# A graph kernel whose six gather passes are fetched by GpSimd alone, through a ring of eight waves

## The reference, cut to what matters

```python
# L0, four steps: one row of a table of 3125*4 rows for each edge, summed by destination, then a GRU
m = (embedding @ W_msg.T + b_msg).reshape(n, 4, 128)
r = segment_sum(m[src, etype], dst)
embedding = gru_cell(r, embedding, ...)
# L1: one row of x for each edge, scaled by a small network of the edge's attributes, summed
x_j = x[src]; msg = pe(edge_w) * x_j + x_j
s = segment_sum(msg, dst) / count
# L2: one row of h for each edge, summed, then a GRU
messages = segment_sum(h[src] @ W_msg.T + b_msg + emb[edge_type], dst)
# L3: attention over the edges: rows of k and v (1 KB together) for each edge, softmax by destination
alpha = softmax_by_dst((q[dst] * (k[src] + e)).sum(-1) / 4)
out = segment_sum((v[src] + e) * alpha, dst)
```

## Time and profile before

| what | value |
|---|---|
| median of 3 runs | 4273.61 us |
| lowest and highest | 4272.66 and 4279.78 us |
| profiled execution, first to last instruction (span) | 6447.3 us |
| GpSimd busy in it | 2764.1 us, 43% |
| TensorE busy in it | 2897.1 us, 45% |
| VectorE, ScalarE busy in it | 1811.8 us and 443.4 us |
| granted TensorE clock | 0.699 of 2.4 GHz |

### The profile page before, as it was taken

One profiled execution on the slowest core, in us unless ns is written; L12 is line 12 of the kernel. 1 busy time (PEld: TensorE's weight loads), 2 busy tenths in 40 slices (PEclk: granted clock), 3 DMA queues, 4 the chain that ended last, 5 costly groups with the idle time before them and its releaser, 6 DMA issues. The chain is left out here.

```text
span 6447.3 us, 67941 instructions
## 1 busy us (share of the span) xinstructions
PE 2897.1 (45%) x12174; PEld 2182.6 (34%) x12175; DVE 1811.8 (28%) x4739; ACT 443.4 (7%) x719; POOL 2764.1 (43%) x2883
## 2 busy tenths in 40 slices
PE   5443044441064430365632555567444106555578
PEld 3333023331033320133421454455333004545465
DVE  3222021221032220233321322223222005555685
ACT  2000010000010000100000100002000001000133
POOL 4666016663056660166630444452666203665400
PEclk7776567665576665677766678778677557766789
DMA  3111011110011110111110111110111001433331
GB/s 114 47 47 45 3 43 46 46 47 23 3 64 47 47 44 3 39 48 45 45 29 9 46 31 32 31 36 27 43 47 48 18 3 62 128 123 119 97 126 54
DMA packets 167915, 315.16 MB, mean 49 GB/s; under 512 B 63863, under 2 KB 89662, under 8 KB 167138
## 3 DMA queue, kind: packets, MB, share of 16 engines
q0 software_dynamic: 94528, 207.40, 12.3%
q1 hardware_dynamic: 60818, 102.68, 4.7%
q10 hardware_dynamic: 12304, 2.65, 0.2%
HBM read 250.84 MB, written 61.65 MB: 48 GB/s over the span
## 5 line engine op out<-in xcount | busy, mean ns | idle before, releaser
L708 POOL DMA_INDIRECT ring<-m_tab,idx x1536 | 1470.2, 957 | 812.2 <-issue 435.9
L1689 PE MATMUL ps<-oh,ring 128*128 128x256 f32 (+1 forms) x2902 | 885.1, 464 | 1913.3 <-DMA ring<-m_tab 994.8
L1689 PEld LDWEIGHTS ps<-oh,ring 128*128 128x128 f32 x2902 | 640.4, 243 | 2041.1 <-issue 1946.9
L1689 PE MATMUL ps<-nodes,ring 128*128 128x256 f32 (+1 forms) x2766 | 820.9, 454 | 731.7 <-issue 619.8
L1174 DVE TENSOR_SCALAR oh<-iota,dl 128x256 f32<-128x256 f32 x1248 | 386.5, 381 | 2432.4 <-PE ps L1689 1397.4
L708 POOL DMA_INDIRECT ring<-x_tab,idx x768 | 729.5, 950 | 611.7 <-PE ps L1689 311.5
L1689 PEld LDWEIGHTS ps<-nodes,ring 128*128 128x128 f32 x2766 | 593.7, 237 | 844.5 <-issue 759.1
L1174 DVE TENSOR_SCALAR nodes<-iota,dl 128x256 f32<-128x256 f32 x1175 | 364.6, 380 | 982.6 <-remote 913.2
L708 POOL DMA_INDIRECT ring<-kv_tab,idx x416 | 403.5, 970 | 262.8 <-DVE rec L1485 136.5
L728 POOL TENSOR_TENSOR small<-small,bc 128x4 f32<-128x4 f32 (+1 forms) x28 | 29.6, 1056 | 967.1 <-DVE small L1273 967.1
L540 POOL TENSOR_TENSOR ring<-nodes,ring 128x512 f32<-128x512 f32 (+1 forms) x21 | 24.3, 1155 | 897.0 <-ACT ring L820 897.0
(11 more groups left out here) (261 smaller groups left out, 2646.1 us busy)
## 6 DMA issues: line engine op xcount, KB each, us to landing
ring<-m_tab SPq DMA_DIRECT2D x4096, 0.5 KB
ring<-m_tab ACTq DMA_DIRECT2D x4096, 0.5 KB
ring<-x_tab SPq DMA_DIRECT2D x2048, 0.5 KB
ve_dr<-pw SPq DMA_DIRECT2D x52, 512.0 KB
ring<-ve_dr SPq DMA_DIRECT2D x52, 512.0 KB, 3.4
ring<-m_tab,idx POOLq DMA_INDIRECT x1548
m_tab<-ring SPq DMA_DIRECT2D x75, 256.0 KB, 2.2
ring<-x_tab ACTq DMA_DIRECT2D x1024, 0.5 KB
```

Source lines behind the costliest of these rows:

```text
L708: pool.indirect_dma_start(rows[:, j, :], None, table, bass.IndirectOffsetOnAxis(ap=idx[:, wave * WV + j:wave * WV + j + 1], axis=0)).then_ ...
L1689: return T.matmul(o, lhsT, rhs, start=start, stop=stop, skip_group_check=True)
```

## The change

GpSimd gathers all 403 tiles of each of the first six passes. DEPTH becomes 8: waves 0 to 3 of a turn lie in the first halves of the ring's rows, waves 4 to 7 in the second halves, where the far tiles were (function slot, which is not changed, places them). The single rows of SyncE and ScalarE are gone, with their row numbers, their registers, their semaphores and all that waited for them. The loops of VectorE, ScalarE and TensorE over the waves now have bodies of eight waves, run six times, and three waves behind them; the order written by hand is gone. The weights wpad, whose place held the row numbers, are loaded right behind the first table's stores.

```diff
-DEPTH = 4
+DEPTH = 8
 OH_BUFS = 2
-FULL = TILES // WV
-NEAR = FULL * WV
-FAR = P_SLOTS - NEAR
-LAST_SPLIT = 5
-SP_TILES, ACT_TILES = 8, 8
-LOOPED = FULL // DEPTH - 1
+LOOPED = P_WAVES // DEPTH
+P_REST = P_WAVES - LOOPED * DEPTH
...
+IN_SLOT = [16 * sum(tiles_of(wave) for wave in range(s, P_WAVES, DEPTH)) for s in range(DEPTH)]
+
+def landed(k, s, i, n=WV):
+    return k * IN_SLOT[s] + i * (16 * WV) + 16 * n
...
             with eng.Fori(0, LOOPED) as i:
                 for u in range(DEPTH):
                     body(i, u, i * DEPTH + u, WV)
-            for p, wave in enumerate(LAST_POS):
-                body(LOOPED, p, wave, tiles_of(wave))
+            for u in range(P_REST):
+                body(LOOPED, u, LOOPED * DEPTH + u, tiles_of(LOOPED * DEPTH + u))
...
             def first_table(rows):
                 for n in range(WIN):
-                    if n == BY_POOL:
-                        sp.wait_ge(xi_st, 16)
-                        row_numbers(sp, 0)
...
-                sp_rows(sp, m_tab, xrow0)
...
-                waves, deep, slots = (WAVES, RING, SLOTS) if single(k) else (FULL, DEPTH, NEAR)
+                waves, deep, slots = (WAVES, RING, SLOTS) if single(k) else (P_WAVES, DEPTH, P_SLOTS)
...
-                hidden(s, "L0", m_landed(s))
-                act_rows(act, m_tab, xrow0)
+                hidden(s, "L0")
                 evac(s)
...
-            for n, (to, i_) in enumerate(zip(x_bytes, (idx4, idx1))):
-                step(f"i_x{n}", V.tensor_scalar(to, i_[:, NEAR:NEAR + SP_TILES + ACT_TILES], 9, None, ALU.logical_shift_left))
```

More of the change, by code:

```diff
@@ L122, in first_wave, with tiles_of @@
     return k * P_WAVES
[L125 to L139, removed]
+def tiles_of(wave):
+    return P_LAST if isinstance(wave, int) and wave == P_WAVES - 1 else WV
+IN_SLOT = [16 * sum(tiles_of(wave) for wave in range(s, P_WAVES, DEPTH)) for s in range(DEPTH)]
+def landed(k, s, i, n=WV):
+    return k * IN_SLOT[s] + i * (16 * WV) + 16 * n
 class Any1(dict):
@@ L268, in build @@
         credit = sem("credit")
-        gat = [sem(f"gat{i}") for i in range(DEPTH)]
+        gat = [sem(f"gat{i}") for i in range(max(DEPTH, RING))]
         mt_mm = sem("mt_mm")
@@ L313, in build @@
         b_e2 = sem("b_e2")
[L314 to L317, removed]
         s_wpad = sem("s_wpad")
-        gat_end = sem("gat_end")
-        x_sp = [sem(f"x_sp{i}") for i in range(4)]
-        x_ac = [sem(f"x_ac{i}") for i in range(4)]
         b_used = sem("b_used")
@@ L386, in build @@
                  + [yT[:, 1024 * b:1024 * (b + 1)].rearrange("p (s c) -> p s c", c=P) for b in range(2)])
-        x_bytes = [pw[:, 1, 32 * j:32 * j + SP_TILES + ACT_TILES].bitcast(I32) for j in range(2)]
         cntc, inv = small[:, 208:208 + WIN], small[:, 176:176 + WIN]
@@ L406, in slot @@
             return ring[:, s % RING, :, h:h + D]
[L408 to L415, removed]
         def halves(wave):
@@ L425, in split_turns @@
                     body(i, u, i * DEPTH + u, WV)
-            for p, wave in enumerate(LAST_POS):
-                body(LOOPED, p, wave, tiles_of(wave))
-        X_SP, X_AC = (n * P // 4 * 16 for n in (SP_TILES, ACT_TILES))
-        def far_slot(t):
-            return ring[:, t // WV, t % WV, D:2 * D]
+            for u in range(P_REST):
+                body(LOOPED, u, LOOPED * DEPTH + u, tiles_of(LOOPED * DEPTH + u))
         def wave_rows(wave, u):
-            if isinstance(wave, int) and wave >= FULL:
-                return ring[:, wave - FULL, :, D:2 * D]
@@ L439, in wave_rows @@
             return slot(wave % DEPTH if isinstance(wave, int) else u)
[L441 to L493, removed]
@@ L498, in arrived @@
                 eng.wait_ge(gat[u], landed(k, u, i))
[L499 to L508, removed]
+            else:
+                eng.wait_ge(gat[wave % DEPTH], landed(k, wave % DEPTH, wave // DEPTH, tiles_of(wave)))
         def logit_turns(eng, body):
@@ L529, in whole_turns @@
         def whole_turns(eng, turn):
-            with eng.Fori(0, LOOPED - 1) as i:
+            with eng.Fori(0, LOOPED) as i:
                 turn(i, [i * DEPTH + u for u in range(DEPTH)])
-            turn(LOOPED - 1, L1_POS)
+            turn(LOOPED, [LOOPED * DEPTH + u for u in range(P_REST)])
         def new_state(unit, eng, r, c, h_in, h_out):
@@ L613, in _ @@
             first_table(m_rows)
[L614 to L617, removed]
-                sp_rows(sp, m_tab, xrow0)
[L619 to L622, removed]
+            sp.dma_start(wpad_flat, a["wpad"]).then_inc(s_wpad, 16)
+            for s in range(1, STEPS):
+                table(s, m_rows, 512)
             def rows_out(ln):
@@ L635, in rows_out @@
                     sp.dma_start(dst, buf).then_inc(ln_dma[c % 2], 16)
[L637 to L641, removed]
             rows_out(0)
@@ L645, in _ @@
                 sp.dma_start(dst, src).then_inc(s_w2 if j else s_w1, 16)
-            for c in range(2):
-                sp.wait_ge(ln_dma[c], LN_DMA(1, c))
-            sp_rows(sp, x_tab[0], xrow)
             rows_out(1)
-            for c in range(2):
-                sp.wait_ge(ln_dma[c], LN_DMA(2, c))
-            sp_rows(sp, x_tab[1], xrow)
             table(STEPS, kv_rows, 2 * D)
@@ L710, in gathers @@
                             bass.IndirectOffsetOnAxis(ap=idx[:, wave * WV + j:wave * WV + j + 1], axis=0)
[L711 to L715, removed]
-                                bass.IndirectOffsetOnAxis(ap=idx[:, NEAR + t:NEAR + t + 1], axis=0)).then_inc(x_l1, 16)
-                    if slots == NEAR and g == (FULL - 1 if k == PASS_L1 else LOOPED * DEPTH - 1):
-                        for t in range(SP_TILES + ACT_TILES, FAR):
-                            pool.indirect_dma_start(
-                                far_slot(t), None, table,
-                                bass.IndirectOffsetOnAxis(ap=idx[:, NEAR + t:NEAR + t + 1], axis=0)).then_inc(x_pl, 16)
+                        ).then_inc(gat[u], 16)
             def norm(ln):
@@ L797, in evac, with hidden @@
                     nc.scalar.activation(gT[:, c0:c0 + cw], ps[:, c, 0:cw], ACT.Copy).then_inc(ev_a, 1)
-            def m_landed(s):
-                def f():
-                    for b in range(RING):
-                        act.wait_ge(mt_dma[b], (s + 1) * (16 * MT_SLOTS[b]))
-                return f
-            def hidden(r, L, landed=None):
+            def hidden(r, L):
                 parts = len(hid[L])
@@ L808, in hidden @@
                     c0, cw = CH[n // parts]
-                    if n == parts * NCH - 1 and landed:
-                        landed()
                     act.wait_ge(hid_mm, r * (3 * NCH) + (n + 1))
@@ L853, in _ @@
                     gru(s, "L0", c)
-            hidden(STEPS - 1, "L0", m_landed(STEPS - 1))
-            act_rows(act, m_tab, xrow0)
+            hidden(STEPS - 1, "L0")
             evac(STEPS - 1)
@@ L896, in _ @@
             hidden(STEPS, "L2")
-            act.wait_ge(xi_ld, 64)
-            for c in range(2):
-                act.wait_ge(ln_dma[c], LN_DMA(2, c))
-            act_rows(act, x_tab[1], xrow)
             evac(PASS_L2)
@@ L1371, in messages @@
                         arrived(dve, PASS_L1, i, u, wave)
-                        if hf and isinstance(wave, int) and wave == FULL - 1:
-                            all_arrived(dve, PASS_L1)
                         dve.wait_ge(l1_pe, (i * DEPTH + u) * 2 + (hf + 1))
@@ L1752, in wave @@
                     for j in range(n):
-                        if isinstance(g, int) and g == FULL - 1 and j == LAST_SPLIT:
-                            all_arrived(pe, k)
                         ins = mm(psf[:, ds(cs[j], PAIR)], wave_rows(g, u)[:, j, :], pair_oh(u, j), start=False, stop=False)
```

11 lines of the change are left out of this document (removed).

## The result

The changed kernel takes 4366.32 us (median of 4 runs, 4362.91 to 4369.01), the kernel before 4276.06 in the same comparison: a ratio of 1.0211, 95% interval 1.0197 to 1.0226, or +90.3 us. The prediction was 4363, in a range of 4285 to 4405.

What follows compares the result with a forecast made beforehand. GpSimd's back-to-back gathers were taken to bound the passes: 4273.6 + 97.8 for 80 more gathers in L0 and L2 - 8.9 at the start = 4362.5, say 4363 us, in a range of 4285 to 4405.

Steps and rivals of the forecast that it cites:

- GpSimd bounds the passes: All passes without a profile: GpSimd issues gathers back to back; 80 more in L0 and L2 cost +97.8 us.
- The step by which I got 1.223: Price of a gather: median 4273.6 less 916.3 us of other work, over 2746 gathers, gives 1.223 us each.
- The two rules of the Trainium skill: Rules against the sum: descriptor generation is small, and issuing from several engines saves little; overlapping gathers would add almost nothing.
- L1's eight gathers at nothing: L1: 8 more gathers cost 0, hidden by the engines' 10.7 us chain per wave against 10.0 of gathers.
- Single rows at 0: Queues of SyncE and ScalarE: rows are in time, so removing them gains 0; up to 34 us kept for the low end.
- some 17 us late in the first pass: ScalarE's single rows, first pass: done after 490 us, against 473 us of gathers, so perhaps some 17 us late.
- The start, -8.9: First table's stores: without SyncE's stop for row numbers, the last store and first gather come 8.9 us sooner.
- The ring of eight at 0: GpSimd may be 64 gathers ahead in place of 32: taken as 0, with -37 us as the bound.
- The pause every second wave: GpSimd's pauses of about 3 us, read as the profile's; their vanishing would mean the ring was too short.
- its pauses and its late rows: First profile: 839 us of GpSimd pauses and TensorE's waits for single rows, taken as absent from the timed executions.
- The span of about 5310: New profile of the changed kernel: span expected near 5310 us, from 6447.3 with the waits for rows gone.

Runs made afterwards that it cites:

- e3: Kernel before, with ScalarE's 8 far tiles gathered by GpSimd in L0 and L2 too, SyncE's left as single rows: 4322.12 us, ratio 1.01.
- e8: Kernel before with the edits of e6 and e7, plus a ninth tile of single rows on SyncE, one gather less per pass: 4325.67 us, ratio 1.0115.
- e5: Kernel before, unchanged, profiled a second time: 4275.81 us, span 4274.0 us.
- e2: Kernel before, each far tile of SyncE and ScalarE fetched by one plain transfer of 128 consecutive rows, not single rows: 4273.56 us, ratio 0.9989.
- e4: Kernel before, with SyncE's reading back of row numbers moved behind the first table's last store: 4274.53 us, ratio 0.9993.
- e7: Kernel before with e4's edit, and ScalarE's writing of row numbers moved behind the landing of the table: 4274.08 us, ratio 0.9995.
- e1: Changed kernel with DEPTH = 4, a ring of four waves in place of eight: 4369.01 us, ratio 1.0209.
- e12: Kernel of e10 again, unchanged, on a chip of the usual kind: 4262.17 us, ratio 0.9959.
- e6: Kernel before, with SyncE's far wave of L1 taken behind wave 41 in place of wave 43: 4277.75 us, ratio 1.0.
- e10: Kernel before with e7's start, e6's L1 order, and SyncE's far wave first in the other passes' last turn: 6525.47 us, 1.0042, on the slow chip.
- e9: Kernel of e2 with far waves ahead of the last gathered ones in every pass: 5064.06 us, ratio 0.7806, on the slow chip.

## Why the prediction was right, and where its steps were not

*GpSimd bounds the passes.* Right, and shown by e3 and the windows: 1.25 us for each gather in both kernels, and a time that grows with their number. e8 shows the limit: with one tile more on SyncE the passes no longer end with the gathers. The step by which I got 1.223 was not sound. It took 916.3 us of other work from the trace; in e5 the time outside the gathers is 4274.0 - 3452.7 = 821.3 us, and (4273.6 - 821.3)/2746 = 1.257. The rows of 1.25 were the better price. The two rules of the Trainium skill that spoke against the sum (DMA: Bandwidth & Descriptors, "Anatomy of one DMA — SWDGE (gpsimd) path" and "Issuing engines are not separate DMA queues") are not borne out by these traces: 88 more gathers made 109.4 us of stretches (99.5 + 9.9), 1.24 us each, with the DMA engines busy 0.20 of the time. What the engine that issues saves is its own time, as the second rule says, but here that time is not small: it bounds the pass.

*L1's eight gathers at nothing.* Wrong, by 9.9 us. The 10.7 us of the earlier trace rows is a wave whose first half ran slowly (2.07 and 3.40 us, where the second half has 1.16 and 1.89). In e5 TensorE is behind the gathers at the end of L1 and waits for none of them, and there one wave follows the other like this (timeline of TensorE):

```profile
2730.67 1.16 PE L1689 MATMUL ps<-rts,wpad 128*128 128x128 f32 x8 [0.85 <-DVE ring L1376]
...
2739.99 1.16 PE L1689 MATMUL ps<-rts,wpad 128*128 128x128 f32 x8 [0.85 <-DVE ring L1376]
```

That is 9.3 us for a wave, its turns with VectorE and ScalarE included, under the 10.0 of its gathers. The prediction had named this case at 10 us.

*Single rows at 0.* Right: e2 gives 5 us, with an interval that begins at 0.9 (0.9998). The rates from the idle queue, 0.407 and 0.425, were the right ones to take; the trace of e5 has 0.414 and 0.437. I had ScalarE's rows some 17 us late in the first pass; they end 12 us ahead of the last gather (538.95 and 550.7). Most of this difference is their start: 25 us behind SyncE's in e5 (91.31 and 66.56), where I had taken 55 from the first profile. The gathers also take 484.6 us in place of the 473 that I set against them, and the rows 448 in place of 435. The margin is small all the same: one more tile on SyncE costs 48 us (e8).

*The start, -8.9.* It is -6.8. Taking the read away from between the stores alone gave 1.2 us (e4), and only moving the write as well gave 5.8 (e7). I had counted the stop of SyncE as the whole of it.

*The ring of eight at 0.* Right on the usual chips (e1: 4369.01 against 4366.32). The pause every second wave did vanish from the new profile, which the prediction had named as a sign that the ring was too short. It is no such sign: e5 and e1 have four waves and no pause either.

*The tails.* Missing from the prediction, -13.5 us. TensorE must take three far waves between the last gathered ones, and I had costed that order at nothing. e1 and e2 show that neither the depth nor late rows make it, and e12 that the order does in L0 and L2. In L1, where the changed kernel gains 6.0 us, one other order was tried with single rows, in two kernels (e6, e12: 14.4 and 15.7 us), and it did not shorten the tail as the change did. The rows of e5 above suggest why, but no run tests it, so the cause stays open. Up to SyncE's far wave VectorE, and with it TensorE, waits some 4.7 us in most waves for gathered rows, the last time until 2683.23 us; behind it neither waits for rows again. That wave is 9.3 us of work with no gathers of its own, and each of the five full waves that follow makes up only 10.0 - 9.3 = 0.7 us. By this estimate some 6 us are left at the end, as measured, and taking the wave two waves sooner brings 1.4, which e6 shows (1.2) and e12 does not.

*The two misses in price cancel.* +9.9 in L1 and -13.5 in the tails lie beside +1.7 on the gathers and +2.1 on the start. That the forecast lay within 3.3 us of the measured time is in part luck. (2.5 of the 3.3 are the kernel before, 4276.06 us here against the 4273.61 that I started from.)

*What the first profile shows.* I read its pauses and its late rows as the work of the profile. That was wrong: on one chip the runs themselves take as long as that trace and look like it (e10), and elsewhere a profiled execution takes as long as the others (e5). That the runs of 4273.6 us could not look like that trace was right, and the forecast rested on this; that GpSimd issues without a pause in them was inferred, and e5 then showed it. The span of about 5310 that I expected of the new profile was wrong, 4364.1: it priced executions of the first profile's kind, in which the changed kernel was never seen.

## What to carry to other kernels

Compare the span of a trace with the median of the runs first, and where they differ by half, ask for a second trace before pricing anything: the one count that survived here was the interval of an instruction whose engine never waits. Where one engine issues back to back through a whole pass, the time is its number of instructions times its interval, so work handed to idle queues is worth nearly its full price (43 of 50 us in e3), up to the point at which they hold up the pass; one tile past that point cost 48 us where its six gathers saved 7.5. And what stands behind the last item of the bounding engine is a term of its own: put the waves that other queues bring ahead of the last gathered ones, as far as their landing allows.

## What the runs showed of the hardware

- A gather of 128 rows of 512 bytes took GpSimd 0.95 us, with 0.30 us before the next, on the chip of e9 and e10 as on the others, and with single rows beside it or without. Rows of 1 KB took 0.97 (402.75/416 and 403.18/416).
- A transfer of one row of 512 bytes cost SyncE's queue 0.414 us, its share of loading row numbers into registers included, with gathers beside it (e5). On one chip of five it was 1.59 us as long as GpSimd gathered (e10).
- On that chip VectorE stood still for 22.7 us at a time while GpSimd issued gathers, and went on some 4 us after GpSimd had stopped. The same kernel took 6496.51 us there and 4277.3 to 4278.7 us on the other four, each within 0.4%. Whether the chip or its state at that time makes the difference is not shown.
